# A fused gated-linear-attention and expert layer: q, k and v|gate projected as three products of rounded parts, the next sequence's transposes at a step's end

## The chip, the cores and the metric

One core of one Trainium2 chip. The metric is the device time of one launch in microseconds (us); a run of the kernel before and one of the changed kernel are compared on the same chip. The engines are TensorE (PE, with its weight loads as PEld), VectorE (DVE), ScalarE (ACT), GpSimd (POOL) and the queue of SyncE (SP), which issues most DMAs.

## The reference, cut to what matters

```python
x = x + attn(layernorm(x))            # 8 sequences, T = 512 tokens, D = 256, f32
x = x + ffn(layernorm(x))
# attn:
q = silu(x @ wq); k = sigmoid(x @ wk); v = x @ wv; f = 1 - k
g = log(f); theta = cumsum(sign(f - 0.5)) * pi
# q, k rotated by theta, two heads of 128; S = S*exp(g) + k v^T; o = q S / sqrt(2*128), token by token
out = o * sigmoid(x @ wg1 @ wg2)
out = (out - mean) * rsqrt(var + eps) * norm_w;  out @ wo
# ffn: each token goes to the one of 8 experts with the largest affinity; layernorm, 256 -> 1024 relu -> 256,
# alpha = sigmoid(affinity); out = alpha * y + (1 - alpha) * x
```

The scan over tokens is computed in chunks of 128 tokens: within a chunk by seven levels of pairwise halves, between chunks by a state.

## The kernel before

`build_program` writes one instruction stream for each engine by hand, with semaphores; `need(engine, semaphore, per, step, k)` is a wait. Every engine executes its own list in order, so a position in the list is a position in time.

**Attention is a software pipeline of nine steps.** In step i, `step(a, b, c, nxt)` works on four sequences at once: a (number i) is projected, b (i - 1) goes through the levels and its outputs, c (i - 2) is projected by `wo`, added to x, and prepared for the experts, nxt (i + 1) is normalised. Steps 0 and 1 and the last have some of these missing.

**The level stage.** For each of 7 levels l and 2 heads h: ACT copies keys into `k_mix` (`mix`), PE multiplies (`level`, L978), DVE multiplies queries and keys by decays (`update`, L1328), and up to level 4 DVE copies scores under a mask (`pick`, L1339). `level` of l + 1 waits for the `mix` of l + 1 and for the pick of l - 1, `mix` of l + 1 for the `update` of l. Between two such products PE has a filler that belongs to a or c: `k_proj`, `q_proj` (`channels`, L990), `o_transposes`, `out_proj`. DVE has `decays` (L1489) and `q_mult` (L1494) of a between its updates.

**The second stage of a step.** After the last `level`, PE has `q_proj(a, 1, 1)`, `g1_proj(a)`, `k_transposes(b)` (L1043), `key_values(b)` (L1056), `v_proj(a)` (L1019), `gate_proj(a)` (L1028), `x1_transposes(c)` (L1103), `diagonal(a)` (L1035), `outputs(b)` (L1070, L1071) with the affinity products (L1111) between. DVE has `residual` (L1505), `q_mult(a, 1)`, statistics, `states`, then `gating` (L1530) and `route` of c (L1369 to L1383). POOL has `decay_tree` (L657), `qk` (L662), the two normalisations and the product of queries with the decays (L676). ACT ends a step with `x_norm` of nxt (L759), `mix(a, 0, ·)`, the eight `rows_of(c)` (L849, L852) and `alphas`.

**The head of a step.** PE: `level(b, 0, 0)`, `transposes(a)` (L985, two groups of four 128x128 into `bank_a0` and `bank_a1`), `level(b, 0, 1)`, `ranks`, `k_proj(a)`. ACT: `xn_copy(a, 0)`, `mix(b, 1, 0)`, `xn_copy(a, 1)`, `mix(b, 1, 1)`; xn_copy is a 128x512 copy by L732. DVE: the four updates of level 0, `sums` and `moments` of c, then level 1.

An f32 product is two matmul instructions in the trace (x4 is two products). In the listings of instruction order it is one row.

**The experts** follow: 39 tiles of 128 tokens; `up` (L1215) and `down` (L1231), and from tile 12 on `down_in_parts`: the weights and the activations rounded to float32r (`w2_high`, `h_high`) with the rest in `w2_low`, `h_low`, and three products in place of one f32 product (L1245, L1246, L1250). This stage is not changed.

## Time and profile before

| | us |
|---|---|
| median of 3 runs | 609.88 |
| lowest, highest | 609.61, 614.47 |
| the profiled execution | 613.98 |
| its span | 612.2 |
| PE busy in it | 568.2 |
| DVE busy in it | 432.9 |
| ACT busy in it | 341.8 |
| POOL busy in it | 313.1 |

The span is from the first to the last instruction; 1.8 us of the execution lie around it. The attention steps fill it from 0 to about 319 us, the experts the rest. `level(b, 0, 0)` of steps 1 to 8 starts at 32.63, 65.61, 101.6, 138.04, 174.47, 211.8, 249.15 and 286.19 us. In a timeline row stand the start, the length, the engine, the line, and in brackets how long the engine was idle before and whose result ended that. The engine's pitch is the distance between two starts; a row's length also has the time until its result is there. A matmul's end is modelled.

### The profile page before, as it was taken

To read this page: it belongs to the slowest core of one execution; us is meant where nothing else is said; L and a number is where in the kernel's file an instruction comes from. 1 tells how busy PE (TensorE), PEld (TensorE's weight loads), DVE (VectorE), ACT (ScalarE), POOL (GpSimd) and SP (SyncE) were. 2 spreads that over 40 slices of the span, in tenths; PEclk is the share of its full clock that TensorE was granted. 3 is DMA by queue.
4 is the path that set the end of the run, shared out by engine and by line. 5 is a ranking of instruction groups with operands and counts; after the bars stand their busy time and mean duration, and the time that the engine had idled before them with its cause. 6 is when DMAs were issued, how large, how long until landed. Compare 5 with 4: busy or idle time off the path is not lost.

```text
span 612.2 us, 12947 instructions
## 1 busy us (share of the span) xinstructions
PE 568.2 (93%) x3854; PEld 490.3 (80%) x3854; DVE 432.9 (71%) x990; ACT 341.8 (56%) x754; POOL 313.1 (51%) x390
## 2 busy tenths in 40 slices
PE   2988999999999999999779999999999999999991
PEld 1556778687777867777669998999999999999990
DVE  1396895969779597898672445435888888888880
ACT  3464758768586775856564342224565565565550
POOL 7715244564725548253613425335767767767721
PEclk9999999999999999999699999999999999999996
DMA  8920111121112011020469447556765665665400
GB/s 300 417 94 0 35 36 35 70 70 60 46 35 76 30 69 36 13 92 2 124 213 347 168 160 256 190 190 208 231 217 193 225 228 190 239 224 195 142 6 0
DMA packets 25188, 83.61 MB, mean 137 GB/s; under 512 B 3821, under 2 KB 13423, under 8 KB 18992
## 3 DMA queue, kind: packets, MB, share of 16 engines
q1 hardware_dynamic: 16896, 59.57, 27.6%
q0 software_dynamic: 7552, 22.89, 11.4%
q8 instruction: 24, 0.39, 0.3%
q10 hardware_dynamic: 688, 0.52, 0.3%
q14 instruction: 28, 0.23, 0.1%
HBM read 70.35 MB, written 13.53 MB: 137 GB/s over the span
## 4 chain that ended last, share of the span: by engine, by line
PE 81%; DVE 8%; issue 4%; POOL 3%; DMA 2%; ACT 1%; DVEq 0%; ACTq 0%; POOLq 0%
PE bank_a L1215 21%; PE bank_a L990 8%; PE bank_l L978 7%; PE bank_l L1231 6%; PE bank_l L1250 4%; PE bank_l L1245 4%; PE bank_l L1246 4%; PE bank_c L1094 4%; PE bank_a L1019 4%; DVE arena L1328 3%; PE bank_b L1071 3%; PE bank_a L1035 2%; PE bank_a L1028 2%; PE bank_b L1070 2%; PE bank_c L1111 2%
## 5 line engine op out<-in xcount | busy, mean ns | idle before, releaser
L1215 PE MATMUL bank_a<-masks,arena 128*128 128x128 f32 x1248 | 145.9, 275 | 0.0
L1215 PEld LDWEIGHTS bank_a<-masks,arena 128*128 128x128 f32 x1248 | 143.4, 192 | 0.5
L1328 DVE TENSOR_TENSOR arena<-arena 128x256 f32<-128x256 f32 x224 | 92.1, 456 | 12.4 <-PE bank_l L978 11.0
L978 PEld LDWEIGHTS bank_l<-arena,k_mix 128*128 128x128 f32 x448 | 65.2, 197 | 43.7 <-ACT k_mix L732 27.4
L1627 DVE TENSOR_TENSOR arena<-bank_a,b_col 128x512 f32<-128x512 f32 x78 | 53.9, 691 | 63.9 <-PE bank_a L1215 52.7
L683 POOL DMA_INDIRECT arena<-rows_by_expert,take_idx x39 | 47.7, 1223 | 81.7 <-DVE k_mix L1641 79.3
L978 PE MATMUL bank_l<-arena,k_mix 128*128 128x128 f32 x448 | 72.9, 288 | 10.6 <-DVE arena L1339 7.3
L990 PE MATMUL bank_a<-arena 128*128 128x512 f32 x160 | 82.0, 611 | 0.0
L732 ACT ACTIVATE k_mix<-arena 128x128 f32<-128x128 f32 x224 | 60.4, 308 | 35.7 <-DVE arena L1328 30.7
L911 ACT ACTIVATE masks<-bank_b,b_col,g_col 128x128 f32<-128x128 f32 x78 | 31.4, 454 | 60.4 <-PE bank_b L1203 60.4
L1647 DVE TENSOR_TENSOR w_low<-w_sb,w_high 128x2048 fp32r<-128x2048 f32 x27 | 61.9, 2293 | 3.7 <-issue 2.8
L689 POOL TENSOR_SCALAR put_of<-arena,skip 128x1 int32<-128x1 f32 x39 | 61.7, 1583 | 1.0
L921 ACT ACTIVATE h_high<-arena 128x512 fp32r<-128x512 f32 x54 | 31.1, 623 | 53.8 <-PE bank_l L1250 51.2
L657 POOL TENSOR_TENSOR arena<-arena 128x512 f32<-128x512 f32 (+6 forms) x56 | 27.5, 490 | 59.4 <-DVE arena L1489 55.6
L695 POOL DMA_INDIRECT out<-k_mix,put_of x39 | 41.4, 1063 | 24.2 <-DVE k_mix L1641 13.5
L1245 PE MATMUL bank_l<-w_high,h_high 128*128 128x256 f32 x216 | 53.0, 288 | 0.8 <-ACT h_high L921 0.8
L732 ACT ACTIVATE w_high<-w_sb 128x2048 fp32r x27 | 51.2, 1895 | 0.0
L1246 PE MATMUL bank_l<-w_low,h_high 128*128 128x256 f32 x216 | 50.6, 277 | 0.0
L1231 PE MATMUL bank_l<-w_sb,arena 128*128 x192 | 43.7, 381 | 1.3 <-issue 1.3
L732 ACT ACTIVATE arena<-bank_a 128x512 f32<-128x512 f32 x40 | 23.8, 594 | 34.5 <-PE bank_a L1019 28.5
L631 POOL DMA_INDIRECT rows_by_expert<-arena x32 | 33.5, 1048 | 16.6 <-issue 16.6
L1245 PEld LDWEIGHTS bank_l<-w_high,h_high 128*128 128x128 f32 x216 | 40.6, 188 | 1.0 <-issue 1.0
(160 smaller groups left out, 1079.4 us busy)
## 6 DMA issues: line engine op xcount, KB each, us to landing
arena<-w SPq DMA_DIRECT2D x39, 1024.0 KB
arena<-x SPq DMA_DIRECT2D x16, 512.0 KB, 3.5
w_sb<-w SPq DMA_DIRECT2D x8, 1024.0 KB, 14.8
arena<-b SPq DMA_DIRECT2D x1, 1024.0 KB
arena<-rows_by_expert,take_idx POOLq DMA_INDIRECT x39
out<-k_mix,put_of POOLq DMA_INDIRECT x39
rows_by_expert<-arena POOLq DMA_INDIRECT x32
arena<-wk SPq DMA_DIRECT2D x1, 256.0 KB, 4.0
```

Source lines behind the costliest of these rows:

```text
L683: pool.indirect_dma_start(out=gathered[p].bitcast(I32), out_offset=None, in_=rows, in_offset=bass.IndirectOffsetOnAxis(ap=take_idx[:, n:n ...
L689: pool.tensor_scalar(put_of[:, n:n + 1], gathered[p][:, 2 * D + 1:2 * D + 2], skip[:, n:n + 1], None, ALU.add).then_inc(s_put, 1)
L732: return act.activation(dst, src, ACT.Copy)
L978: ins = pe.matmul(bank, k_mix[l % 2][:, m * P:(m + 1) * P], level_queries(buf, m, l), start=True, stop=True)
L990: return pe.matmul(bank[:, :], w[:, i * width + h * P:i * width + (h + 1) * P], xn_t[:, i * T:(i + 1) * T], start=(i == 0), stop=(i == DC ...
L1215: m = pe.matmul(bank_a[k // 4][:, k % 4 * P:(k % 4 + 1) * P], w1_now[t.par][:, i * F + k * P:i * F + (k + 1) * P], xl_t[t.par % 2][:, i * ...
L1231: m = pe.matmul(bank_l[p][:, 0:D], h_act[:, k * P:(k + 1) * P], w2_sb[:, bass.ds(e * (FC * D) + k * D, D)], start=(k == 0), stop=(k == FC ...
L1245: pe.matmul(bank_l[p][:, 0:D], h_high[:, h], w2_high[p][:, w], start=(k == 0), stop=False)
L1246: pe.matmul(bank_l[p][:, 0:D], h_high[:, h], w2_low[p][:, w], start=False, stop=False)
L1328: dve.tensor_tensor(half, half, factor(decay[b.par], h, l, second), ALU.mult).then_inc(s_up, 1)
L1627: dve.tensor_tensor(h_sb[:, n * 512:(n + 1) * 512].rearrange("p (k t) -> p k t", t=P), bank_a[n][:, :].rearrange("p (k t) -> p k t", t=P), ...
L1647: dve.tensor_tensor(w2_low[t.par % 2], w2_of(e), w2_high[t.par % 2], ALU.subtract).then_inc(s_wlo, 1)
```

## The change

- `xn_copy` writes a rounded (float32r) `xn_high`, and DVE computes `xn_low = bank_a - xn_high` (`xn_low_part`). `wk`, `wq` and the joined v|gate weights are split into high and low parts once, at the start. `wg1 @ wg2` is multiplied once at the start and takes the place of the gate's two products.
- `channels` issues three 128x512 float32r matmuls for one f32 product. `v_gate(a, j)` computes v and gate of 128 tokens together, 128x512, in six; four of these take the place of `g1_proj`, `v_proj` and `gate_proj`. Their results leave by eight ACT operations of 128x256 in place of five of 128x512.
- The transposes move from the head of step i + 1 to the end of step i, behind `outputs(b, 1)`; ACT's `xn_copy(nxt, 0)` comes between the fourth and the fifth of the eight `rows_of(c)`, `xn_copy(nxt, 1)` behind the last. On DVE `xn_low_part(nxt, 0)` ends the step, `xn_low_part(a, 1)` stands between the two updates of level 0.
- x1 is made in place of the residual's x, and x1's transpose in place of `o_t`; so SP loads `x_res` of b at the end of its step's list, after `rows_of(c)`, and in the last step behind the four first expert weights.
- In step 0 POOL's decay tree comes behind the queries' product, and ACT's `mix(a, 0, ·)` ahead of `x_norm`.

```diff
         def _(sp):
...
-                if b is not None:
-
-                    need_apart(sp, s_x1, 2, b, 0)
-                    sp.dma_start(tiles(x_res), seq_rows(x_t, b)).then_inc(s_xres, 16)
                 if a is None:
...
+                if b is not None:
+
+                    if number(b) == 0:
+                        sp.wait_ge(s_mask, 2)
+                    need_apart(sp, s_zn, TJ, b, 0)
+                    need_apart(sp, s_base, TJ, b, 0)
...
+                    sp.dma_start(tiles(x_res), seq_rows(x_t, b)).then_inc(s_xres, 16)
...
                 if a is not None:
+                    if b is not None:
+                        decay_tree()
...
                     pool.tensor_tensor(queries(kq[a.par]), q_raw.rearrange("p (m s) -> p m s", s=2 * P),
...
+                    if b is None:
+                        decay_tree()
...
-                copy(xn_t[:, i * T:(i + 1) * T], bank_a[i][:, :]).then_inc(s_xnt, 1)
+                copy(xn_high[:, i * T:(i + 1) * T], bank_a[i][:, :]).then_inc(s_xnt, 1)
...
-                of(c, rows_of)
+                if b is None:
+                    of(nxt, x_norm)
+                of(c, rows_of, range(2))
+                of(nxt, xn_copy, 0)
+                of(c, rows_of, range(2, TJ))
+                of(nxt, xn_copy, 1)
                 of(c, alphas)
...
-                return pe.matmul(bank[:, :], w[:, i * width + h * P:i * width + (h + 1) * P], xn_t[:, i * T:(i + 1) * T],
-                                 start=(i == 0), stop=(i == DC - 1))
+            def channels(high, low, h, bank, i):
...
+                pe.matmul(bank[:, :], high[:, w], xn_high[:, x], start=(i == 0), stop=False)
+                pe.matmul(bank[:, :], low[:, w], xn_high[:, x], start=False, stop=False)
+                return pe.matmul(bank[:, :], high[:, w], xn_low[:, x], start=False, stop=(i == DC - 1))
...
+            def v_gate(a, j):
+
+                if j < 2:
+                    need(pe, s_q, H, a, j + 1)
                 else:
+                    need(pe, s_v, TJ, a, j - 1)
+                    need(pe, s_gate, TJ, a, j - 1)
+                for i in range(DC):
+                    x = slice(i * T + j * P, i * T + (j + 1) * P)
+                    w = slice(i * 2 * D, (i + 1) * 2 * D)
+                    pe.matmul(bank_a[j % 2][:, :], xn_high[:, x], wvg_high[:, w], start=(i == 0), stop=False)
+                    pe.matmul(bank_a[j % 2][:, :], xn_high[:, x], wvg_low[:, w], start=False, stop=False)
+                    m = pe.matmul(bank_a[j % 2][:, :], xn_low[:, x], wvg_high[:, w], start=False, stop=(i == DC - 1))
+                m.then_inc(s_vg, 1)
...
                 of(b, level, 0, 0)
-                of(a, transposes, 0)
-                of(a, transposes, 1)
                 of(b, level, 0, 1)
...
-                of(a, g1_proj, 0)
+                of(a, v_gate, 0)
                 of(b, k_transposes)
-                of(a, g1_proj, 1)
+                of(a, v_gate, 1)
                 of(b, key_values)
-                of(a, v_proj, 0)
-                of(a, v_proj, 1)
-                of(a, gate_proj, 0)
+                of(a, v_gate, 2)
...
                 of(c, x1_transposes)
-                of(a, gate_proj, 1)
+                of(a, v_gate, 3)
                 of(a, diagonal, 0)
...
                 of(b, outputs, 1)
+                of(nxt, transposes, 0)
+                of(nxt, transposes, 1)
...
+            def xn_low_part(a, i):
+                need(dve, s_tp, DC, a, DC)
+                need(dve, s_xnt, DC, a, i + 1)
+                x = slice(i * T, (i + 1) * T)
+                dve.tensor_tensor(xn_low[:, x], bank_a[i][:, :], xn_high[:, x], ALU.subtract).then_inc(s_xlo, 1)
...
                     of(b, update, l, 0)
+                    if l == 0 and b is not None:
+                        of(a, xn_low_part, 1)
...
                 of(c, route)
+                of(nxt, xn_low_part, 0)
                 if b is None:
```

Where the lists change at the seam between two steps: DVE before, from the second `gating` of b (L1530) over `route` of c to level 0 of the next step (L1328 is `update`, L1303 and L1309 are statistics).

```order
L1530 SCALAR_TENSOR_TENSOR arena<-bank_b1,arena 128x512
L1369 TENSOR_TENSOR arena<-aff,aff_best 128x32
L1371 SCALAR_TENSOR_TENSOR arena<-arena,iota_e 128x32
L1374 TENSOR_REDUCE arena<-arena 128x4
L1378 COPY arena<-arena 128x8
L1380 SCALAR_TENSOR_TENSOR arena<-iota_e,arena 128x4x8
L1383 SCALAR_TENSOR_TENSOR arena<-arena 128x40
L1328 TENSOR_TENSOR arena<-arena 128x4x64 x4
L1303 BN_STATS o_stat<-arena 128x6 x2
L1309 BN_AGGR o_mom<-o_stat 128x2 x4
```

And now, in the same place, from the end of `route` (L1434) on; L1369 is now `xn_low_part` and L1379 `update`.

```order
L1434 SCALAR_TENSOR_TENSOR arena<-arena 128x40
L1369 TENSOR_TENSOR xn_low_49<-bank_a0,xn_high_50 128x512
L1379 TENSOR_TENSOR arena<-arena 128x4x64 x2
L1369 TENSOR_TENSOR xn_low_49<-bank_a1,xn_high_50 128x512
L1379 TENSOR_TENSOR arena<-arena 128x4x64 x2
L1348 BN_STATS o_stat<-arena 128x6 x2
L1354 BN_AGGR o_mom<-o_stat 128x2 x4
```

Two subtractions are new, one ahead of the updates of level 0 and one between them. ACT at the same seam before (L849 and L852 are `rows_of`, the last rows `alphas`, `xn_copy` and `mix`):

```order
L849 ACTIVATE arena<-arena,u_shift,u_rstd 128x256
L852 ACTIVATE arena<-arena,u_shift,base_scale 128x256
L837 ACTIVATE arena<-aff_best 128x4
L732 ACTIVATE arena<-arena 128x4
L732 ACTIVATE arena<-bank_a0 128x512
L732 ACTIVATE k_mix1<-arena 128x64x2 x2
L732 ACTIVATE arena<-bank_a1 128x512
L732 ACTIVATE k_mix1<-arena 128x64x2 x2
```

And ACT there now (L873, L876: `rows_of`; L758: copies):

```order
L758 ACTIVATE xn_high_50<-bank_a0 128x512
L873 ACTIVATE arena<-arena,u_shift,u_rstd 128x256
L876 ACTIVATE arena<-arena,u_shift,base_scale 128x256
L873 ACTIVATE arena<-arena,u_shift,u_rstd 128x256
L876 ACTIVATE arena<-arena,u_shift,base_scale 128x256
L758 ACTIVATE xn_high_50<-bank_a1 128x512
L861 ACTIVATE arena<-aff_best 128x4
L758 ACTIVATE arena<-arena 128x4
L758 ACTIVATE k_mix1<-arena 128x64x2 x4
```

Four of the eight `rows_of` now stand behind the first copy of the transposes and ahead of the second. DVE in step 0, from the second diagonal (L1396) to the first updates, has the cast of the masks (L1660) behind the new subtraction:

```order
L1396 TENSOR_TENSOR arena<-bank_a0,ident 128x512
L1396 TENSOR_TENSOR arena<-bank_a1,ident 128x512
L1369 TENSOR_TENSOR xn_low_49<-bank_a0,xn_high_50 128x512
L1660 CAST masks<-arena 128x3584
L1379 TENSOR_TENSOR arena<-arena 128x4x64 x2
```

Before, the cast (L1605) followed the second diagonal at once and had no transposes ahead of it.

## Rows read from the trace of the kernel before

**Rows 1.** page: busy time by engine, and chain that ended last
```profile
PE 568.2 (93%) x3854; PEld 490.3 (80%) x3854; DVE 432.9 (71%) x990; ACT 341.8 (56%) x754; POOL 313.1 (51%) x390
...
PE 81%; DVE 8%; issue 4%; POOL 3%; DMA 2%; ACT 1%; DVEq 0%; ACTq 0%; POOLq 0%
```

**Rows 2.** windows: length, busy us of each engine, granted clock, DMA
```profile
142.27:158.59 16.32, 16.18 (x84) 11.33 (x82) 15.57 (x41) 11.90 (x37) 8.76 (x12) 1.00 0.19 67
158.59:174.47 15.88, 15.88 (x102) 13.41 (x101) 9.68 (x32) 11.30 (x27) 10.33 (x17) 1.00 0.20 67
174.47:178.70 4.23, 4.16 (x29) 3.33 (x28) 3.93 (x18) 3.18 (x10) 0.00 (x0) 1.00 0.00 0
42.00:50.00 8.00, 5.63 (x32) 4.01 (x31) 8.00 (x23) 5.61 (x19) 0.21 (x1) 1.00 0.00 0
288.00:300.00 12.00, 8.76 (x39) 7.93 (x40) 9.95 (x31) 7.21 (x22) 6.15 (x9) 0.58 0.17 66
```

**Rows 3.** timeline of DVE, 139 to 160 us: start, length, instructions, idle
```profile
139.92 1.41 DVE L1328 TENSOR_TENSOR arena<-arena 128x256 f32<-128x256 f32 x4
...
142.27 0.76 DVE L1328 TENSOR_TENSOR arena<-arena 128x256 f32<-128x256 f32 x2
...
147.97 0.76 DVE L1328 TENSOR_TENSOR arena<-arena 128x256 f32<-128x256 f32 x2 [0.29 <-PE bank_l L978]
...
157.14 1.52 DVE L1328 TENSOR_TENSOR arena<-arena 128x256 f32<-128x256 f32 x2 [0.41 <-PE bank_l L978]
158.59 1.28 DVE L1505 TENSOR_TENSOR arena<-bank_c,arena 128x512 f32<-128x512 f32 x2
159.78 0.68 DVE L1494 TENSOR_TENSOR arena<-bank_a,arena 128x512 f32<-128x512 f32 x1
```

**Rows 4.** timeline of PE in the same step, 156 to 175 us
```profile
156.94 1.88 PE L990 MATMUL bank_a<-arena 128*128 128x512 f32 x4
...
160.37 1.58 PE L1056 MATMUL bank_b<-arena 128*128 128x128 f32 x12
161.78 3.62 PE L1019 MATMUL bank_a<-arena 128*128 128x256 f32 x16
...
166.10 1.04 PE L1103 MATMUL bank_c<-ident,arena 128*128 128x128 f32 x8
...
168.70 0.39 PE L1071 MATMUL bank_b<-arena 128*128 128x128 f32 x2
...
174.47 0.62 PE L978 MATMUL bank_l<-arena,k_mix 128*128 128x128 f32 x4
```

**Rows 5.** timeline of ACT in the same step
```profile
139.14 0.60 ACT L732 ACTIVATE arena<-bank_a 128x512 f32<-128x512 f32 x1
...
171.33 0.59 ACT L849 ACTIVATE arena<-arena,u_shift,u_rstd 128x256 f32<-128x256 f32 x1
171.82 0.59 ACT L852 ACTIVATE arena<-arena,u_shift,base_scale 128x256 f32<-128x256 f32 x1
```

**Rows 6.** timeline of PE in the expert stage, products of rounded parts
```profile
440.79 0.28 PE L1245 MATMUL bank_l<-w_high,h_high 128*128 128x256 f32 x1
440.90 0.28 PE L1246 MATMUL bank_l<-w_low,h_high 128*128 128x256 f32 x1
```

**Rows 7.** timelines of DVE and PE, end of step 1, start of step 2
```profile
49.63 2.68 DVE L1328 TENSOR_TENSOR arena<-arena 128x256 f32<-128x256 f32 x4
...
65.61 0.62 PE L978 MATMUL bank_l<-arena,k_mix 128*128 128x128 f32 x4
...
69.31 0.76 DVE L1328 TENSOR_TENSOR arena<-arena 128x256 f32<-128x256 f32 x2
```

**Rows 8.** timeline of all engines at the start of the program
```profile
22.13 3.48 POOL L657 TENSOR_TENSOR arena<-arena 128x512 f32<-128x512 f32 x7 [3.78 <-DVE arena L1489]
...
29.99 2.08 ACT L759 ACTIVATE arena<-arena,x_shift,x_rstd 128x256 f32<-128x256 f32 x4 [0.47 <-POOL x_shift L601]
...
31.40 2.75 DVE L1605 CAST masks<-arena 128x3584 uint8<-128x3584 f32 x1
```

More of the change, by code:

```diff
@@ L145, in build_program @@
         x_sb = [lay.take(TJ * D) for _ in range(2)]
-        xn = lay.take(TJ * D)
-        xn_t = lay.take(DC * T)
+        xn_low = lay.take_rounded("xn_low", DC * T)
+        xn = arena[:, lay.at - DC * T:lay.at]
+        xn_high = lay.take_rounded("xn_high", DC * T)
         q_raw = lay.take(H * T)
         qk = lay.take(H * T)
-        g1_t = lay.take(T)
         kq, decay, v_sb, gate, attn_t = ([None, None] for _ in range(5))
@@ L174, in build_program @@
         x_res = lay.take(TJ * D)
-        x1 = lay.take(TJ * D)
-        x1_t = lay.take(DC * T)
+        x1 = x_res
+        x1_t = o_t
         wo_sb = lay.take(DC * D)
@@ L839, in alphas, with rows_of @@
                 copy(tiles(row_sb, RW)[:, :, 2 * D + 1], ids[:, n * TJ:(n + 1) * TJ]).then_inc(s_alpha, 1)
-            def rows_of(c):
+            def rows_of(c, js=range(TJ)):
                 need(act, s_shift["u"], 1, c, 1)
@@ L847, in rows_of @@
                     act.wait_ge(s_row_out[n > EARLY], 16 * TJ * (n - EARLY if n > EARLY else n))
-                for j in range(TJ):
+                for j in js:
                     act.activation(tiles(row_sb, RW)[:, j, 0:D], tiles(x1)[:, j], ACT.Identity,
@@ L937, in turn @@
                     gains(before(t, -2))
+            act.wait_ge(s_wk, 16)
+            copy(wk_high, wk_sb).then_inc(s_whigh, 1)
+            act.wait_ge(s_wq, 16)
+            copy(wq_high, wq_sb).then_inc(s_whigh, 1)
             x_norm(Step(0, 0, 2))
+            act.wait_ge(s_w1t, 1)
+            copy(wg1_t, bank_b[1][:, 0:DC * P]).then_inc(s_w1tc, 1)
+            for i in range(DC):
+                xn_copy(Step(0, 0, 2), i)
+            act.wait_ge(s_wv, 16)
+            copy(vg_half(wvg_high, 0), wv_sb).then_inc(s_whigh, 1)
+            act.wait_ge(s_w12, 1)
+            copy(vg_half(wvg_high, 1), bank_b[0][:, :].rearrange("p (c n) -> p c n", c=DC)).then_inc(s_whigh, 1)
             pipeline(act, step)
@@ L1023, in gate_proj @@
-            def gate_proj(a, half):
-                need(pe, s_g1, 1, a, 1)
-                need(pe, s_v, 2, a, half + 1)
-                for j in range(2):
-                    t0 = (2 * half + j) * P
-                    m = pe.matmul(bank_a[1 - half][:, j * D:(j + 1) * D], g1_t[:, t0:t0 + P], wg2_sb[:, :], start=True, stop=True)
-                m.then_inc(s_gz, 1)
+            def v_gate(a, j):
+                if j < 2:
+                    need(pe, s_q, H, a, j + 1)
+                else:
+                    need(pe, s_v, TJ, a, j - 1)
+                    need(pe, s_gate, TJ, a, j - 1)
+                for i in range(DC):
+                    x = slice(i * T + j * P, i * T + (j + 1) * P)
[4 more added lines that the diff above has]
+                m.then_inc(s_vg, 1)
@@ L1031, in diagonal @@
             def diagonal(a, h):
                 need(pe, s_qk, 1, a, 1)
[L1034 to L1035 removed]
+                need(pe, s_v, TJ, a, h + 3)
+                need(pe, s_gate, TJ, a, h + 3)
+                pe.matmul(bank_a[h][:, :], ones[:, :], qk[:, h * T:(h + 1) * T], start=True, stop=True).then_inc(s_dz, 1)
             def k_transposes(b):
@@ L1264, in _ @@
             pe.wait_ge(s_const, 1)
-            pe.wait_ge(s_wqk, 32)
+            pe.wait_ge(s_wg, 32)
+            for i in range(DC):
+                m = pe.transpose(bank_b[1][:, i * P:(i + 1) * P], wg1_sb[:, i * P:(i + 1) * P], ident[:, :])
+            m.then_inc(s_w1t, 1)
+            for i in range(DC):
+                transposes(Step(0, 0, 2), i)
+            pe.wait_ge(s_w1tc, 1)
+            for i in range(DC):
+                m = pe.matmul(bank_b[0][:, i * D:(i + 1) * D], wg1_t[:, i * P:(i + 1) * P], wg2_sb, start=True, stop=True)
+            m.then_inc(s_w12, 1)
+            pe.wait_ge(s_whigh, 2)
+            pe.wait_ge(s_wlow, 2)
             pipeline(pe, step)
```

150 lines of the change are left out of this document (82 added, 68 removed).

## The prediction

> **What bounds the kernel now.** I read the busy times and the chain that ended last first: PE is busy for 93% of the span and has 81% of that chain [rows 1]. That speaks for any cut of PE's work. Then I cut one middle step (start 138.04, next start 174.47, so 36.43 us) into three windows [rows 2]: the level stage from the first update of level 1 to the end of the last update (142.27 to 158.59, 16.32 us), the second stage (158.59 to 174.47, 15.88), and the head of the next step up to its first update of level 1 (174.47 to 178.70, 4.23). PE is full in all three, but it is not alone: DVE is busy 15.57 of the 16.32 us of the level stage and 3.93 of the 4.23 of the head, and only 9.68 of the second stage. The timeline of DVE shows what this means: it waits 0.29 and 0.41 us in the level stage, 0.70 in all [rows 3]. So two engines bound the levels, PE and DVE, and PE alone bounds the second stage. The experts' stage, 293 us, isn't touched.
>
> **PE's work.** A row's length has the last result's latency in it: the keys' products last 1.58 from 160.37, and the next row starts at 161.78, 0.17 before their end. An f32 128x512 product is two instructions; the two from 156.94 are 1.88 less 0.17, 0.86 us each. v is eight products of 256 columns, 3.62 less 0.17, so 3.45, and the gate's four 1.73 [rows 4]. Before: (4 + 4 + 2) x 0.86 + 3.45 + 1.73 = 13.8 us for each sequence. A float32r product of 256 columns starts 0.11 after the one before it [rows 6], so I take 0.22 for 512 columns, an estimate: the trace has none. After: 24 x 0.22 for k and q and 24 x 0.22 for v|gate, 10.5 us. PE saves 3.3 us for each of 8 sequences, 26 us. Bounds from the nearest rows: 0.22 (the 0.11 doubled) and 0.43 (an f32 instruction of 512 columns, half of 0.86); I take the first, since it is the same kind of product. The Trainium skill ("TensorE: Matmul & The Clock Gate", section Back-to-back issue gap) gives N/2.4 + 2.5 ns when warm, 216 ns for 512 columns; by it PE would save 3.4 us.
>
> **Second stage.** Count from D, the end of the last update. `v_gate(a, 1)` waits for `q_mult(a, 1)`, which DVE does only after both residuals: they start at 158.59 and it starts at 159.78 [rows 3], with its 0.6 and a signal it is done at D + 1.9. Before, g1 and the keys' products lay there and PE waited for nothing. PE then has v_gate(1) 1.3, `key_values` 1.4 (160.37 to 161.78), v_gate(2) 1.3, x1 transposes 0.87, v_gate(3) 1.3, the diagonal 0.86, and both outputs with affinities and diagonal(1) 5.77 (168.70 to 174.47) [rows 4]: 12.8. It ends at D + 14.7 in place of 15.88: 1.2 us saved. What ACT adds, eight operations of 128x256 at some 0.4, lies beside PE: v_gate(2) needs those of v_gate(0), done during `key_values`. POOL's list is unchanged there.
>
> **Head.** Before, 4.23. After, the way from the end of outputs(1) to the first update of level 1 runs through ACT. The first four transposes and their signal take 0.66: the copy started at 139.14 [rows 5], 1.10 behind level 0's start at 138.04, and level 0's product is half the length of the eight transposes' 0.87 (166.10 [rows 4], less the latency). Then xn_copy(0) 0.5; then the second four `rows_of`, which start every 0.49 (171.33, 171.82 [rows 5]), 1.97; xn_copy(1) 0.6 with its signal; xn_low(1) 0.68, like other DVE reads of a bank [rows 3]; the second pair of updates of level 0, 0.7; sums and moments of c, 1.03 (139.92 + 1.32 to 142.27 [rows 3]). The sum is 6.1, 1.9 more than before. DVE alone would need gating 0.7, route 1.1, 2 x 0.68, updates 1.4 and 1.03, 5.6; so ACT's order is the last to come, by half a microsecond. The two new subtractions and the four rows are the price here. Net, second stage and head: +0.7 us a step.
>
> **Level stage.** DVE's work in it is the same. Faster fillers can only take away its waits: of the 0.29 I leave 0.2 (the product of level 3 waits for a pick of DVE too), of the 0.41 I take it all. So 16.32 becomes 15.8, -0.5. A `need` is not removed, and `q_proj` now only makes PE wait longer. Here 8 x 0.2 us of PE's saving disappear.
>
> **First steps.** Step 0: POOL's tree took 3.48 us ahead of everything that leads to x_norm at 29.99 and level 0 at 32.63 [rows 8]; it moves behind. Bounds: 3.5 us gained, or 1 lost. What is late next: x_norm of 2.08 us must now be followed by transposes (0.64), a copy (0.6) and xn_low(0) (0.7) before DVE may begin the cast of the masks, 2.75 us, which before began at 31.40 with no such wait [rows 8]. I put x_norm at about 27.9 (the last gate copy at 27.0, then four mix 0.9), the cast at 31.8 and its end at 34.4, where it stood at 34.1. I take 0 for step 0, near the row of the cast. The copies and subtractions of the weights lie in the time before x_shift at 8.5, or beside PE.
>
> Step 1 has no c, so no rows stand between the copies and no residual ahead of q_mult. Before, from the end of the last update (49.63 + 2.68 = 52.3) to the first update of level 1 at 69.31 it is 17.0, with step 2 starting at 65.61 [rows 7]. After: v_gate(1) at D + 0.8, key_values to 3.5, v_gate(2), v_gate(3), diagonal to 7.0, outputs 1.35, diagonal, outputs to 10.9, transposes and two copies (ACT is free from x_norm and mix at 11.3) to 12.7, then xn_low, update, sums and moments: 15.9. Gain 1.1.
>
> **The sum.** Level stages of steps 1 to 7: -0.2 - 6 x 0.5 = -3.2. Second stage and head after steps 2 to 6: 5 x 0.7 = +3.5. After step 1: -1.1. Step 7 has no nxt, so only its second stage counts: -1.2. Step 0: 0. In all -2.0. The profiled execution of 613.98 would be 612.0; it lies 4.1 above the median, so against the median of 609.88 I predict 607.9, say 608. The last step is bound by updates, mixes and picks in turn and is not changed; that SP starts the first expert weights some 20 us earlier hides nothing that PE waits for now.
>
> **Rivals.** (1) PE bounds the levels after all, as its share of 93% and the chain say [rows 1]: then every step gets its 3.3 us back, 26 us, 584; half of it, 597. Against it: DVE's two waits are all the slack there is. (2) Step 0 shortens by the tree, because x_norm comes earlier than I put it: another -3.5, 604.4. Against it: the cast. (3) Slower: ACT's order decides and PE's second stage doesn't shrink, since each v_gate(j) waits for two copies of j - 2 and v_gate(1) for q_mult. The place is the seam of steps 2 to 6; the price is the head's +1.9 five times and nothing back in levels or second stage, +9.5, 619. It decides once copies last over the 1.3 us of a v_gate. (4) The clock: in the last step, where PE waits for DVE in each level, the granted clock over 288 to 300 is 0.58 [rows 2], between its levels of 1.2 and 2.4 GHz; with seven level stages like that, each with some 6 us of level products at half rate, it is over 40 us more, 650. For it: PE is to wait more in the levels. Against it: from 42 to 50 us PE is busy 5.63 of 8.00 and the clock stays at 1.00 [rows 2]; I expect it above that. The Trainium skill warns of this (the same page, section HAM oscillation): a matmul kernel that idles between bursts falls back to the lower clock; the last step agrees, the window of step 1 doesn't. (5) The change doesn't do what it says: 512 columns of float32r take 0.43, then 48 x 0.43 = 20.6 in place of 13.8, +6.8 a step, +55, 664.
>
> **How the numbers follow.** A measurement of this kernel can tell about 1% from no change, 6.1 us: 603.8 to 616.0. My case 0.56, all within. Rival 1: 0.18, faster. Rival 2: 0.12, of which 0.04 beyond 1%. Rival 3: 0.10, slower. Rivals 4 and 5: 0.04 together, slower. So faster 0.22, same 0.64, slower 0.14. The range for 8 in 10 holds my case with its own error of half a microsecond a step (604 to 612), rival 2, the upper half of rival 1's small versions and the lower of rival 3: 601 to 615.
>
> **What would show it.** Right: a step near 36.6 us; DVE's waits in a level stage under 0.4 us, PE's bracketed waits for picks and mixes longer; PE busy down by over 20 us and the span by 2; the copy of the second four transposes about 3.7 us behind the end of outputs(1); the cast of the masks in step 0 starting after 31 us. Wrong: steps of 33 to 35 us with DVE waiting as before (rival 1); level 0 of step 1 with its updates before 31 us (rival 2); v_gate(2) and v_gate(3) waiting for ACT (rival 3); a granted clock under 1 in steps 1 to 7 (rival 4); a spacing of 0.43 for 512 columns (rival 5).

## The result and the profile after

| | us |
|---|---|
| kernel before, median of 20 runs on that chip | 612.24 (609.09 to 615.4) |
| changed kernel, median of 20 runs | 615.51 (613.72 to 620.31) |
| ratio, 95% interval | 1.0062 (1.0045 to 1.0079) |
| the profiled execution, its span | 615.85, 614.1 |

The change makes the kernel 0.6% slower. The unchanged pair, run again on two more chips (runs after_again and after_third), has the ratios 1.0071 (1.0051 to 1.0092) and 1.0064 (1.0038 to 1.0091). The forecast was 0.3% faster.

The page after, busy times and chain that ended last (against [rows 1]):

```profile
PE 553.1 (90%) x3892; PEld 501.6 (82%) x3892; DVE 443.5 (72%) x1010; ACT 343.0 (56%) x783; POOL 311.9 (51%) x390
...
PE 73%; DVE 14%; issue 5%; ACT 3%; DMA 2%; POOL 2%; DVEq 0%; ACTq 0%; POOLq 0%
```

PE lost 15 us of work and DVE gained 10.6. In these two traces the end came 1.9 us later, and 8 points of the chain went from PE to others, 6 of them to DVE.

The windows of step 4, cut at the same instructions as in [rows 2]: level stage, second stage, head of the next step.

```profile
144.62:160.75 16.13, 14.54 (x89) 12.31 (x88) 15.42 (x40) 12.02 (x37) 8.70 (x12) 1.00 0.32 106
160.75:175.78 15.03, 14.32 (x95) 12.18 (x94) 9.82 (x32) 9.72 (x26) 10.44 (x17) 1.00 0.00 1
175.78:181.87 6.09, 5.27 (x37) 4.24 (x35) 5.22 (x19) 4.54 (x13) 0.00 (x0) 1.00 0.24 70
```

Before, these were 16.32, 15.88 and 4.23, 36.43 in all; now 37.25. PE, once all but full in all three, is idle for 1.6, 0.7 and 0.8 us of them. The timelines show where. DVE in the head and the level stage:

```profile
140.41 0.67 DVE L1369 TENSOR_TENSOR xn_low<-bank_a,xn_high 128x512 fp32r<-128x512 f32 x1
...
142.31 0.69 DVE L1369 TENSOR_TENSOR xn_low<-bank_a,xn_high 128x512 fp32r<-128x512 f32 x1 [0.57 <-ACT xn_high L758]
...
150.32 0.76 DVE L1379 TENSOR_TENSOR arena<-arena 128x256 f32<-128x256 f32 x2 [0.29 <-PE bank_l L1018]
...
159.28 1.55 DVE L1379 TENSOR_TENSOR arena<-arena 128x256 f32<-128x256 f32 x2 [0.39 <-PE bank_l L1018]
```

The two subtractions are new, the second waits for ACT's copy, and both waits of [rows 3] are still there (0.29 and 0.39 for 0.29 and 0.41). The eight transposes that now end the step (PE), and ACT's copy of the second four, behind four `rows_of`:

```profile
138.53 1.04 PE L1025 MATMUL bank_a<-ident,arena 128*128 128x128 f32 x8
```

```profile
141.63 0.58 ACT L758 ACTIVATE xn_high<-bank_a 128x512 fp32r<-128x512 f32 x1
```

PE in the levels and the second stage:

```profile
146.72 0.68 PE L1018 MATMUL bank_l<-arena,k_mix 128*128 128x128 f32 x4 [1.23 <-DVE arena L1390]
...
153.75 1.07 PE L1129 MATMUL bank_c<-arena 128*128 128x256 f32 x4
...
161.16 0.82 PE L1078 MATMUL bank_b<-ident,arena 128*128 128x128 f32 x6
162.69 0.50 PE L1060 MATMUL bank_a<-wvg_high,xn_high 128*128 128x512 f32 x1 [0.71 <-DVE arena L1545]
...
164.18 1.50 PE L1091 MATMUL bank_b<-arena 128*128 128x128 f32 x12
```

PE's saving in the fillers is now a wait for a pick of DVE (1.23), and v_gate(1) waits for q_mult. Before, PE's idle time in the whole level stage was 0.14 us (16.32 less 16.18), and none in the second stage (15.88 of 15.88).

In step 1 the granted clock (TensorE's clock as a share of full speed, the third number from the end) falls twice (windows, the changed kernel's first trace):

```profile
34.00:36.00 2.00, 0.88 (x6) 0.83 (x7) 2.00 (x6) 0.85 (x3) 0.00 (x0) 0.99 0.32 67
36.00:38.00 2.00, 2.00 (x8) 1.68 (x7) 2.00 (x5) 1.34 (x5) 0.00 (x0) 0.50 0.59 208
38.00:40.00 2.00, 2.00 (x9) 1.73 (x8) 0.83 (x3) 0.58 (x2) 0.00 (x0) 0.66 0.00 0
50.00:52.00 2.00, 2.00 (x8) 1.69 (x8) 2.00 (x4) 1.21 (x5) 1.34 (x2) 0.50 0.00 0
52.00:54.00 2.00, 2.00 (x8) 1.52 (x8) 1.85 (x4) 1.14 (x3) 1.69 (x5) 0.74 0.00 0
```

### The profile page after: what moved, and what is told of

It reads as the page before. It is cut to its first block, busy times and chain, and to the rows that moved or that the text cites. A ratio compares the mean times of both kernels' runs of the same rounds, so it can differ in the third digit from the quotient of the medians.

```text
span 614.1 us, 13164 instructions
## 1 busy us (share of the span) xinstructions
PE 553.1 (90%) x3892; PEld 501.6 (82%) x3892; DVE 443.5 (72%) x1010; ACT 343.0 (56%) x783; POOL 311.9 (51%) x390
## 4 chain that ended last, share of the span: by engine, by line
PE 73%; DVE 14%; issue 5%; ACT 3%; DMA 2%; POOL 2%; DVEq 0%; ACTq 0%; POOLq 0%
PE bank_a L1249 22%; PE bank_l L1018 6%; PE bank_l L1265 6%; PE bank_c L1129 4%; PE bank_l L1284 4%; PE bank_l L1279 4%; PE bank_l L1280 4%; DVE arena L1379 4%; DVE arena L1390 3%; PE bank_b L1106 2%; PE bank_a L1060 2%; PE bank_a L1062 2%; PE bank_a L1061 2%; PE bank_a L1070 2%; PE bank_b L1105 2%
## 5 line engine op out<-in xcount | busy, mean ns | idle before, releaser
L1249 PE MATMUL bank_a<-masks,arena 128*128 128x128 f32 x1248 | 147.6, 277 | 0.0
L1249 PEld LDWEIGHTS bank_a<-masks,arena 128*128 128x128 f32 x1248 | 145.0, 194 | 0.5
L1379 DVE TENSOR_TENSOR arena<-arena 128x256 f32<-128x256 f32 x224 | 91.2, 450 | 9.6 <-PE bank_l L1018 9.5
L758 ACT ACTIVATE k_mix<-arena 128x128 f32<-128x128 f32 x224 | 61.1, 310 | 40.5 <-DVE arena L1379 39.6
L715 POOL TENSOR_SCALAR put_of<-arena,skip 128x1 int32<-128x1 f32 x39 | 59.2, 1519 | 1.2
L758 ACT ACTIVATE w_high<-w_sb 128x2048 fp32r x27 | 51.2, 1895 | 0.0
L1280 PEld LDWEIGHTS bank_l<-w_low,h_high 128*128 128x128 f32 x216 | 40.7, 188 | 0.0
L1265 PEld LDWEIGHTS bank_l<-w_sb,arena 128*128 128x128 f32 x192 | 35.5, 190 | 5.6 <-issue 1.3
```

Of the source, the lines that this page charges most:

```text
L715: pool.tensor_scalar(put_of[:, n:n + 1], gathered[p][:, 2 * D + 1:2 * D + 2], skip[:, n:n + 1], None, ALU.add).then_inc(s_put, 1)
L758: return act.activation(dst, src, ACT.Copy)
L1249: m = pe.matmul(bank_a[k // 4][:, k % 4 * P:(k % 4 + 1) * P], w1_now[t.par][:, i * F + k * P:i * F + (k + 1) * P], xl_t[t.par % 2][:, i * ...
L1265: m = pe.matmul(bank_l[p][:, 0:D], h_act[:, k * P:(k + 1) * P], w2_sb[:, bass.ds(e * (FC * D) + k * D, D)], start=(k == 0), stop=(k == FC ...
L1280: pe.matmul(bank_l[p][:, 0:D], h_high[:, h], w2_low[p][:, w], start=False, stop=False)
L1379: dve.tensor_tensor(half, half, factor(decay[b.par], h, l, second), ALU.mult).then_inc(s_up, 1)
```

## The experiments

**How they are compared.** One number is the same in all traces of a kernel within 0.02 us: the time from the first `o_mom` of step 2 to that of step 3 (DVE's aggregation at the head of a step). It spans a level stage, a second stage and a head with rows of c, before the disturbance told of below. It is 36.47 to 36.48 for the kernel before (four traces) and 37.23 to 37.24 for the changed one (three). I call it the marker. It is one step of several: on chips with the disturbance the next steps scatter (cast_first, step 3: 37.97 us in one trace and 37.30 in the other), so what a variant does to the whole is read from its ratio too. The ratios are to the kernel before on the same chip, with 95% intervals.

**q_first**: DVE's order in a step.

```diff
                 level(6)
+                of(a, q_mult, 1)
                 if c is not None:
                     for half in range(2):
                         residual(c, half)
...
-                of(a, q_mult, 1)
```

> The changed kernel, with q_mult(a, 1) ahead of the two residuals on DVE. My theory: between the end of the last update and the end of outputs(1) PE bounds the step, from the moment that q_mult lets v_gate(1) go. In the changed kernel's step 4 v_gate(1) stands still for 0.71 us; that wait goes, and no other takes its place before the x1 transposes. The second stage is 0.65 shorter in steps 2 to 7: 6 x 0.65 = 3.9 us, 611.6 against 615.5 for the changed kernel. Rival: the residuals and the statistics of x1 come 0.6 later, the affinities and the x1 transposes with them, and the time stays at 615.5 (within 1).

Measured: 0.9968 (0.9940 to 0.9996). The marker is 36.26, 0.97 less than the changed kernel's, where 0.65 was expected. The ratio is some 1% under the changed kernel's, about 6 us, which is 0.97 in each of six steps. v_gate(1) follows the key transposes at once (PE, step 4):

```profile
160.10 0.82 PE L1078 MATMUL bank_b<-ident,arena 128*128 128x128 f32 x6
160.68 0.47 PE L1060 MATMUL bank_a<-wvg_high,xn_high 128*128 128x512 f32 x1
```

The pitch from one to the other is 0.58, where it was 1.53: the gain is 0.95, and the bracket had only 0.71 (it counts from the modelled end of the row ahead, and here the next product starts 0.24 before that end). The rival (late statistics) is out.

**copies_early**: ACT's order.

```diff
                 of(nxt, xn_copy, 0)
+                of(nxt, xn_copy, 1)
                 of(c, rows_of, range(2, TJ))
-                of(nxt, xn_copy, 1)
```

> The changed kernel, with xn_copy(1) directly behind xn_copy(0) on ACT and the last four rows_of behind both. My theory: DVE sets the way from route to the first update of level 1, and it stands still for 0.57 us there because xn_low(1) waits for xn_copy(1). That wait goes: 0.57 in each of five seams, -2.9 us, 612.6. Rival: ACT's total is what counts; mix(1, 0) stands behind all of it as before and starts at the same time, level 1 of PE with it, and the time stays at 615.5 (within 1).

Measured: 1.0013 (0.9993 to 1.0033), marker 36.56, 0.67 less, expected 0.57. DVE's wait is gone:

```profile
141.05 0.67 DVE L1369 TENSOR_TENSOR xn_low<-bank_a,xn_high 128x512 fp32r<-128x512 f32 x1
141.63 0.75 DVE L1379 TENSOR_TENSOR arena<-arena 128x256 f32<-128x256 f32 x2
142.30 0.68 DVE L1369 TENSOR_TENSOR xn_low<-bank_a,xn_high 128x512 fp32r<-128x512 f32 x1
```

So ACT's place for one copy decided, not its total.

**no_low** and **no_low_2**: both calls of `xn_low_part` in the steps are left out, PE's waits for them with them, and the third product of k, q and v|gate reads high and low parts already there; the result lacks the low part of x. Of the edit, one line:

```diff
-                return pe.matmul(bank[:, :], high[:, w], xn_low[:, x], start=False, stop=(i == DC - 1))
+                return pe.matmul(bank[:, :], low[:, w], xn_high[:, x], start=False, stop=(i == DC - 1))
```

> The changed kernel without xn_low in sequences 1 to 7: DVE's two subtractions are left out, and the third product of k, q and v|gate reads the low weights and xn_high a second time, so PE and ACT do the same work as before; the low part of x is left out of the result. It prices DVE's subtractions. My theory: DVE bounds the way from route to the last update, so two subtractions at a pitch of 0.60 and the 0.57 us wait for ACT are worth up to 1.8 us in a seam, of which level 1's wait for mix(1, 0) keeps 0.6: -1.2 us in each of seven seams, about -8, 607.5. Rival: PE or ACT bounds the seam and the subtractions lie beside it: -0 to -2.

> no_low again (without xn_low in sequences 1 to 7, the low part of x left out). Its first trace lay on a chip with stalls. Theory: ratio to the kernel before 0.996 as before; from residual to residual of steps 2 to 5 it takes 36.3 to 36.4 in each, against 37.2 to 37.3 for the changed kernel: 0.9 of the 1.8 that the two subtractions and their wait make, because level 1 then waits for mix(1, 0) on ACT. Rival: without the stalls it is 35.5, and DVE had all of it.

Measured: 0.9960 (0.9935 to 0.9985) and 0.9956 (0.9927 to 0.9986). The marker is 35.37, 1.86 less, but a new wait stands right behind it, at the first update of level 1:

```profile
138.05 0.92 ACT L758 ACTIVATE k_mix<-arena 128x128 f32<-128x128 f32 x4
...
139.37 0.76 DVE L1380 TENSOR_TENSOR arena<-arena 128x256 f32<-128x256 f32 x2 [0.81 <-PE bank_l L1018]
```

From one start of the transposes to the next (97.76 to 134.08 in no_low_2) it is 36.32, against 37.29 in the changed kernel: 0.97 of the 1.86 stay. That is the theory's case: DVE bounds the head, and ACT's mix(1, 0) is 0.8 to 0.9 behind it. By the ratios it is 1.0 to 1.1% under the changed kernel, 6 to 7 us of the 8 expected.

**pe_more**: more work for PE alone.

```diff
                 pe.matmul(bank[:, :], low[:, w], xn_high[:, x], start=False, stop=False)
+                pe.matmul(bank[:, :], low[:, w], xn_low[:, x], start=False, stop=False)
```

> The changed kernel with a fourth product (low weights times xn_low) in each of the eight channel products of k and q: 8 x 0.23 = 1.84 us more PE work for a sequence, spread over the head and the levels. It asks whether PE's time in the levels counts. My theory (DVE bounds them): the extra product hides where PE waits (1.23 and 0.36 us before levels 2 and 3, 0.7 before level 1 and before v_gate(1)), and shows only between levels 3 and 4, where PE runs without a gap: about +0.5 us a step and the full 1.8 in step 0, +5, 620.5. Rival (PE bounds): +1.84 for each of 8 sequences, +14.7, 630.

Measured: 1.0114 (1.0069 to 1.0159), marker 37.63, only 0.40 more for 1.84 us of products. The ratio is 0.4 to 0.5% over the changed kernel's, some 3 us for 8 sequences, where the theory had 5 and the rival 14.7. So in the changed kernel most of the added work falls into PE's waits in the head and the levels, and a fifth of it doesn't: PE and DVE bound this stretch in turn. (Later steps of this one trace are 0.7 to 1.2 us longer than the changed kernel's; it lies on a chip with the disturbance, so the share of the products in that isn't known.)

**cast_first** and **cast_first_2**: the end of step 0 on DVE.

```diff
-                of(nxt, xn_low_part, 0)
                 if b is None:
                     dve.wait_ge(s_mask, 1)
                     dve.tensor_copy(masks[:, :].rearrange(
...
+                of(nxt, xn_low_part, 0)
```

> The changed kernel, with the cast of the masks ahead of xn_low(0) at the end of step 0 on DVE. My theory: DVE is idle for 2.28 us before xn_low(0) in step 0 and then does the cast of 2.05; the cast fits into that idle time nearly whole, even at the 2.75 that it took in the kernel before. Update(0, 0) of step 1 starts 1.6 to 2.0 us earlier than 33.95, and the time falls by as much: 613.7. Rival: step 1 is bound by something else by then (PE waits for mixes, clock), and less than 0.5 is left.

> cast_first again, beside the others on one chip. Its first trace has the o_mom of step 2 at 66.10 in place of 69.73 and a granted clock of 1.00 through step 1, where the changed kernel has 0.50 to 0.74 in two places; but its ratio to the kernel before, 1.0027, is only 0.35 to 0.44% under the changed kernel's 1.0062 and 1.0071. Theory: the 3.6 us of step 1 reach the end, and on a quiet chip it is 612, ratio 1.001 to 1.003. Rival: they are given back at some later place, and the ratio is 1.005 or more.

Measured: 1.0027 (1.0000 to 1.0053) and 1.0046 (1.0017 to 1.0075). These are 0.2 to 0.4% under the changed kernel's ratios, with intervals that overlap theirs. Update(0, 0) of step 1 starts at 32.03 in cast_first, 1.9 us earlier than in the changed kernel's first trace, and there the clock stays up (windows):

```profile
34.00:36.00 2.00, 2.00 (x12) 1.35 (x10) 2.00 (x6) 1.60 (x5) 0.00 (x0) 1.00 0.36 118
36.00:38.00 2.00, 1.78 (x13) 1.50 (x12) 1.71 (x6) 0.94 (x4) 0.00 (x0) 1.00 0.00 0
46.00:48.00 2.00, 1.02 (x7) 0.86 (x8) 2.00 (x6) 1.23 (x5) 0.06 (x1) 1.00 0.00 0
50.00:52.00 2.00, 1.92 (x12) 1.37 (x12) 1.07 (x2) 0.93 (x3) 1.61 (x7) 1.00 0.00 0
```

cast_first_2, the same kernel, has the second of the two falls, and PE is no less busy ahead of it (1.02 of 2 us in both):

```profile
46.00:48.00 2.00, 1.02 (x6) 0.87 (x4) 2.00 (x7) 1.15 (x5) 0.00 (x0) 0.67 0.00 0
48.00:50.00 2.00, 2.00 (x9) 1.79 (x9) 1.89 (x3) 0.98 (x5) 1.56 (x2) 0.50 0.00 0
```

`o_mom` of step 2 starts at 66.10 in cast_first, where the first trace of the changed kernel has 69.73: 1.9 of the 3.6 are the cast, 1.7 the two falls of the clock. This is the gain between these two traces and not that of the move alone: cast_first_2 has 67.17, and the third trace of the changed kernel 67.65. Not all of it reaches the end. Both runs lay on chips with the disturbance told of below. From `o_mom` of step 2 to that of step 8 the two traces take 225.51 and 224.59 us, 3.6 and 2.7 more than the changed kernel on a quiet chip (221.89), while the kernel before loses 2.3 and 2.0 there (221.38 and 221.13 for 219.09). So some 1 us is given back to the stalls. The rival isn't out: the changed kernel itself was never measured on such a chip.

**head_transposes**: transposes, copies and subtractions back at the head of a step, rounded products kept.

```diff
                 of(b, level, 0, 0)
+                if b is not None:
+                    of(a, transposes, 0)
+                    of(a, transposes, 1)
                 of(b, level, 0, 1)
...
-                of(nxt, transposes, 0)
-                of(nxt, transposes, 1)
```

> The changed kernel with transposes, copies and subtractions of the next x back at the head of the step, as in the kernel before; the rounded products stay. It tells what the move alone is worth. My theory: the move gains nothing, since DVE sets the seam and not PE: here ACT has the copies ahead of mix(1, 0) and all rows behind it, DVE never waits for a copy, and the first update of level 1 comes 5.5 us behind the end of outputs(1) in place of 6.1; and in step 0 the cast no longer waits for xn_low(0). Five times 0.6 and 2: 5 us faster than the changed kernel. Rival: the move fills a PE gap that is on the path, and undoing it costs up to 0.87 in each of seven seams, +6.

Measured: 0.9988 (0.9967 to 1.0009), marker 36.63, 0.60 less than the changed kernel, as expected. The move of the transposes costs 0.6 us a step and, up to `o_mom` of step 2, 3.1 us (67.06, against 70.16 for the changed kernel on the same chip). Of these, 2.7 are there at the first update of step 1 (31.51 against 34.22), since the cast no longer waits for a copy; this trace has no fall of the clock in step 1, the other has two. Without the move the change is no loss and still no gain.

**all_three**, **all_three_2** (the moves of q_first, copies_early and cast_first) and **route_first**, **route_first_2** (and one more):

```diff
                     of(diagonal_of, attn_diagonal, 1)
+                    if diagonal_of is not None:
+                        of(affinities_of, route)
                     of(b, gating, 1)
...
-                of(c, route)
```

> The changed kernel with all three moves: q_mult(a, 1) ahead of the residuals, both xn_copy together ahead of the last four rows_of, and the cast of the masks ahead of xn_low(0). If the three waits lie one behind the other in a step, as my theory has it, the gains add up: -3.9, -2.9 and -1.8, 607 against 615.5 for the changed kernel and 612.2 for the kernel before. Rival: one wait takes the place of another, and the sum is under half of it, 611 or more.

> all_three again, on one chip with the others. Theory: its steps 3 to 7 are 35.6 each where nothing stalls, 1.6 under the changed kernel's and 0.8 under those of the kernel before; five such steps, the seam of step 7 and step 1's 3.1 make 8 + 1 + 3, 603 to 604 on a quiet chip, ratio 0.986 to 0.990. Rival: ratio above 0.992.

> All three moves, and on DVE route(c) ahead of gating(b, 1) as well. In the trace with the three moves DVE stands still for 0.60 us before gating(b, 1), since PE isn't done with outputs(1), and then has route, 1.1 us, on its way to the first update of level 1, with no wait between. My theory (DVE bounds that way): route fills the 0.60, and the time falls by 0.5 us in each of five to six seams, -3: 604 against 607. Rival: gating comes 0.5 later and the wait shows elsewhere; no change.

> The version with the three moves and route ahead of gating(b, 1), again, beside the other two on one chip. Ratio to the kernel before 0.985 on the first chip. Theory: 0.983 to 0.989 again, 13 us under the changed kernel, whether this chip stalls or not. Rival: the first result owed some of its gain to a quiet chip; ratio above 0.992.

Measured: all_three 0.9865 (0.9822 to 0.9908) and 0.9905 (0.9869 to 0.9941), marker 35.59 and 35.60, 1.64 less: 0.97 + 0.67, so the waits lie one behind the other. The second ratio is a little over the 0.986 to 0.990 expected and under the rival's 0.992. route_first 0.9854 (0.9817 to 0.9892) and 0.9851 (0.9806 to 0.9896), medians 602.46 and 602.07, marker 35.08 to 35.09: another 0.5, as forecast. It is 1.5% faster than the kernel before. In its head DVE has no wait from route to the statistics:

```profile
169.49 0.24 DVE L1434 TENSOR_TENSOR_SCAN arena<-arena 128x40 f32<-128x40 f32 x1
169.65 0.67 DVE L1582 SCALAR_TENSOR_TENSOR arena<-bank_b,arena 128x512 f32<-128x512 f32 x1
170.40 0.69 DVE L1369 TENSOR_TENSOR xn_low<-bank_a,xn_high 128x512 fp32r<-128x512 f32 x1
```

**The disturbed traces.** The first trace of the kernel before has level stages of 17.2 us in steps 5 and 6, and no trace of the changed kernel has. Was that a gain of the change?

> The kernel before, to have its trace a second time. Its first trace held some 3 us of idle time in steps 5, 6 and 8 that no step of the changed kernel shows (level stages of 17.2 in place of 16.35 us, 2.11 us of DVE in step 8), and its times spread from 609.1 to 615.4. My theory: these stalls come and go with the execution; in an execution near 610 every level stage of steps 2 to 7 is 16.3 to 16.4, and the step 36.43. Rival: they are there each time, and then the changed kernel really has won 0.9 in those steps.

> The changed kernel itself, so that its variants have it on the same chip beside the kernel before, whose median there was 614.6 to 614.9 and not 612.2. By the ratio 1.0062 of the first comparison it should come to 618.5. Its first trace has no stall in the level stages of steps 5 and 6 (16.5 us from the start of the statistics' o_mom to the residual), where the kernel before and the variants have 0.9 to 1.1 us more. My theory: these stalls belong to an execution and not to a kernel, so this trace will have them. Rival: the changed kernel is free of them by its own order, and has 16.5 again.

> The kernel before once more. On the chip of after_again its median was 609.95, on that of the first variants 614.6, and both of its traces so far have stalls in the level stages of steps 5 to 7 and in step 8. If this chip is a quiet one, its trace should have level stages of 16.7 us in all steps (o_mom to residual) and a step of 36.43 to 36.45 throughout, and a time near 610; on a chip that stalls, the 17.5 of steps 5 and 6 again and 613 to 615.

> All three moves, and POOL starts the four indirect stores of rows only once level(b, 4, 1) is done on PE, some 7 us later in each step. It asks where the stalls of 0.9 to 1.1 us at update(b, 4, 0) in steps 5 and 6 come from: they fall between POOL's third and fourth store. Theory: the stores' transfers hold something up that DVE needs; then the stalls at update(b, 4, 0) go or move to where the stores now are. Rival: the stalls are tied to the place in the program and stay at update(b, 4, 0) in steps 5 and 6. The tree on POOL begins up to 1.5 later, which may cost up to as much in a step: the time is read from the level stages alone.

> The kernel before on the chip of after_third, for its trace. On a quiet chip every level stage from o_mom to residual takes 16.7 us and steps are 36.43; on a chip that stalls steps 5 and 6 take 17.5 to 17.6.

> The changed kernel a third time, with a trace of the kernel before from the same chip beside it. Where before_fourth has the stalls of steps 5 to 8, this trace tells whether the changed kernel has them too. Theory A (they belong to a chip or its memory at the time): both traces have them or neither, and the ratio stays at 1.006 to 1.009. Theory B (the changed kernel's order is free of them): only the kernel before has them, level stages here are 16.5 in all steps, and the ratio is lower on such a chip than on a quiet one, 1.003 to 1.006, since the kernel before loses some 3 us.

before_again (ratio 0.9998, 0.9963 to 1.0033) and before_third (0.9990, 0.9964 to 1.0016) have the stalls, on chips where the kernel before takes 613.7 to 615.7; after_again has none, on a chip where it takes 609.95. before_fourth and after_third lay on one chip: neither has a stall, steps 2 to 6 of before_fourth take 36.47 to 36.48 each, and the ratio is 1.0064. Two quiet traces can't part theory A from theory B, which differ on a chip that stalls, and the changed kernel itself was traced on no such chip. What parts them is its variants: on the chip of before_again all six (q_first, copies_early, cast_first, no_low, pe_more, all_three) have the stalls in steps 5 and 6, and on the chip of before_third cast_first_2 and no_low_2 have them (all_three_2 in step 5 only). cast_first differs from the changed kernel by one cast in step 0, and its steps 5 and 6 take 38.42 and 38.39 us, where the changed kernel's take 37.20 to 37.23. So the order isn't free of stalls, and they were no gain of the change: theory A, by kernels next to it. On the other side, before_again's theory that they come and go with the execution is not borne out: of the chips traced more than once, two have them in every trace and two in none, and after_again, which was to show them, doesn't. The same instruction in before_third (DVE, then PE) and before_fourth (DVE):

```profile
184.78 0.68 DVE L1489 SCALAR_TENSOR_TENSOR arena<-arena 128x512 f32<-128x512 f32 x1
186.46 0.76 DVE L1328 TENSOR_TENSOR arena<-arena 128x256 f32<-128x256 f32 x2 [0.99 <-PE bank_l L978]
```

```profile
184.75 0.61 PE L978 MATMUL bank_l<-arena,k_mix 128*128 128x128 f32 x4
185.19 1.02 PE L990 MATMUL bank_a<-arena 128*128 128x512 f32 x2
```

```profile
187.70 0.68 DVE L1489 SCALAR_TENSOR_TENSOR arena<-arena 128x512 f32<-128x512 f32 x1
188.31 0.76 DVE L1328 TENSOR_TENSOR arena<-arena 128x256 f32<-128x256 f32 x2
```

PE had gone on from the level's products at 185.19, and DVE started a microsecond after it could. In cast_first, the same place of step 5 (DVE, then PE, which has gone on at 187.03):

```profile
188.63 0.76 DVE L1379 TENSOR_TENSOR arena<-arena 128x256 f32<-128x256 f32 x2 [1.09 <-PE bank_l L1018]
```

```profile
186.66 0.61 PE L1018 MATMUL bank_l<-arena,k_mix 128*128 128x128 f32 x4
187.03 0.47 PE L1033 MATMUL bank_a<-xn_high,wq_high 128*128 128x512 f32 x1
```

scatter_late is all_three with POOL's four stores of rows some 7 us later in each step. Meant to tell whether those stores do it, it fell on a chip without stalls and says nothing on that. It took 1.0038 (1.0009 to 1.0066), where all_three has 0.9865 and 0.9905, so the late stores cost over 1%. Its marker is 35.57, like all_three's, but its steps 3, 4 and 6 take 37.62, 38.45 and 38.44. The waits of 1.0 us that DVE has in the levels of steps 4 and 6 are no stalls: PE is at the lower level of the clock, after a head in which it waited for ACT (busy 0.90 and 0.77 of 2 us at 136 to 140):

```profile
142.00:144.00 2.00, 2.00 (x8) 1.71 (x8) 1.56 (x5) 1.62 (x6) 0.13 (x1) 0.50 0.65 209
```

The cause of the stalls stays open.

## Why the prediction was wrong

Three steps of the prediction failed, and all three are terms of its sum. In steps 2 to 7 the level stage and the second stage were each put 0.3 us too short, and the gain of 1.1 us in step 1 didn't come.

**The frame held.** DVE and PE together bound the levels, PE the second stage, and ACT's order the head.

**PE's work: mis-sized.** PE busy fell by 15 us and not by 26, nor by the 20 that I gave as the sign. The pitch inside a group of float32r products of 512 columns is 0.22 to 0.24, near the 0.22 that I took, but in a group behind f32 work the second product starts 0.31 to 0.34 after the first. Nearly every group here stands behind f32 work, so three products of `channels` take 0.78 and not 0.66, and a v_gate 1.46 to 1.49 and not 1.3 (1.39 for v_gate(0), behind q_proj). By these pitches it is 8 x 0.78 + 1.39 + 3 x 1.47 = 12.0 us for a sequence in place of 10.5: PE saves 1.8 us and not 3.3. The Trainium skill ("TensorE: Matmul & The Clock Gate", Back-to-back issue gap) has 216 ns for 512 columns as the gap of a single product, and some 131 ns for a stream. The trace has 0.22 to 0.24 us inside a group and 0.25 on the mean of a v_gate: it agrees with the first, and no row here comes near the second.

**Head, +1.9: right.** 6.09 measured, 6.1 forecast. The second copy starts 3.10 behind the end of outputs(1) (138.53 to 141.63), and the terms ahead of it add up to 3.1; the 3.7 that I named as a sign has the copy's own 0.6 in it.

**"I take it all": wrong.** The level stage lost 0.19 us, not 0.5 (16.13 for 15.8). I took the 0.41 for a wait that faster fillers shorten. Ahead of levels 5 and 6 PE's fillers are `out_proj`, which the change leaves as f32; the row at 153.75 is one, 0.91 from its start to the next level's. The releaser was named rightly and its queue not read. That is 0.3 a stage.

**"v_gates 1.3 each": mis-sized.** A v_gate takes 1.46 to 1.49 (162.69 to 164.18). Three make 0.5 more than I had; `key_values` and the x1 transposes were 0.2 shorter. The stage is 15.03 and not 14.7: 0.3 again.

**v_gate(1) at D + 1.9: right (1.94).** I took the new wait for q_mult as given. It costs 0.95 a step, q_first shows, and it is the dearest of the three waits that the variants took away (0.97, 0.67, and 1.9 once).

**Step 1, -1.1: wrong.** What I had left out are falls of the granted clock, which I had priced (rival 4) for seven level stages or none. From the first update of level 0 to `o_mom` of step 2 the first trace of the changed kernel takes 35.8 us with two falls, the first of the kernel before 34.75 with none, and cast_first 34.07 with none. So without falls the changed kernel would have gained 0.7; with them it loses 1.0 between these two traces. But the falls come and go. All three traces of the changed kernel have two (35.8, 35.9 and 34.7 us; the third has one of them ahead of that first update). The kernel before has one in two of its four (36.28 with, 34.75 without). cast_first has none and cast_first_2 one (34.72). On the mean, `o_mom` of step 2 starts at 69.2 us in both kernels, and the gain of 1.1 is simply missing. What tips it isn't shown. Ahead of the first fall PE is busy 0.88 of 2 us at 34 to 36, waiting for updates behind the cast, and the clock is then at 0.50, the lower level; but ahead of the second, cast_first and cast_first_2 are equally busy and only one falls. How often each fall comes in runs without a trace isn't known. Step 0 itself, forecast 0, came out at -0.24 in the first pair and 0 on the mean.

**The sum.** Up to `o_mom` of step 2 I had -1.3, and the traces have 0 on the mean. From there to the experts' first transposes I had -0.7, and on the chip where both kernels have a quiet trace it is +2.9 (247.30 to 250.18). The two terms of 0.3 in each of six steps account for that miss of 3.6. Together +2.9, where the ratios say +3.8 to +4.3. The last microsecond isn't placed: between two traces of one kernel the clock alone moves `o_mom` of step 2 by up to 1.5 us and the experts' start by 1.6.

**The rivals.** Rival 1 is out: PE's work fell by 15 us and the time rose. So is rival 2: step 1's first update came 0.24 earlier in the first pair, on the mean not at all, and not 3.5. Rival 3 had the right side and half of the mechanism: v_gate(1) does wait for q_mult and ACT's order does decide the head, but v_gate(2) and v_gate(3) wait for nothing, and the second stage shrank by 0.85. Rival 4 came true in one place, for 0.7 to 1.7 us in an execution and not 40. Rival 5 is out by the pitch of 0.22 to 0.24.

## What to carry to other kernels

Before PE work is made cheaper, read whose result each wait on the other engine needs and which filler really stands ahead of it; a filler that isn't changed gives nothing back. A change that adds a pass on the second engine and a new wait for it should be laid out as one loop through both engines: here 1.2 us of DVE work in a step, a copy four rows too late and a product behind two residuals made 15 us less PE work worth nothing, and four reorderings without any less work brought back 2% of the kernel. Compare single steps between two fixed instructions: the step from 2 to 3 repeats to 0.02 us where whole runs differ by 5. And trace a kernel more than once before a difference in an early, thinly filled stage is put down to the change: two traces of one kernel differed there by up to 3 us.

## What the runs showed of the hardware that I had not expected

- Some chips, with the same kernel, stall DVE for 0.98 to 1.07 us at the same instruction of steps 5 and 6, and their step 8 is 1.3 to 1.7 longer, 3 to 4 us in all (before, before_again, before_third, against before_fourth). One chip's trace must not be compared step by step with another's.
- The granted clock can fall to 0.50 for 3 to 4 us in one execution of a kernel and not in another. In the kernel before, PE is busy 2.47, 2.46 and 2.47 of 4 us (30 to 34, traces before, before_again, before_fourth); the first stays at 1.00, the other two are at 0.50 from 34 to 36, and the fall costs 1.5 us. In cast_first and cast_first_2 PE is busy 1.02 of 2 us alike, and one falls, for 0.7 us.
- At the start of the experts `up` of tile 0 takes 3.82 us at a granted clock of 1.00, or 5.0 to 5.45 where it is 0.69 to 0.75 over that stretch. The kernel before has both, and so have variants of the changed one; the first traces of the two differ in it by 1.6 us that are not the change's.
